# A normalisation of queries and keys moved from GpSimd to ScalarE: power -0.5 as a logarithm and an exponential

## The reference

```
def _layer(x, wqkv, qs, ksc, wo, lg, lb, w1, b1, w2, b2):
    h = shift_token(x)
    qkv = h @ wqkv
    q, k, v = jnp.split(qkv, 3, axis=-1)
    q, k, v = (to_heads(q), to_heads(k), to_heads(v))     # 8 heads of 64
    q = l2norm(q) * qs
    k = l2norm(k) * ksc
    q, k = rotary_xpos(q, k)
    o = local_attention(q, k, v)                          # windows of 64, looks one back
    x = x + o @ wo
    h = layernorm(shift_token(x))
    a, g = jnp.split(h @ w1 + b1, 2, axis=-1)
    return x + (a * gelu(g)) @ w2 + b2
```

## Time and profile before

| | |
|---|---|
| median of 3 runs | 2177.14 us (2174.58 to 2178.0) |
| profiled execution | 2163.13 us |
| its span, first to last instruction | 2161.4 us |
| granted TensorE clock, mean | 0.977 |
| busy: PE, DVE, ACT, POOL | 1991.7, 1773.1, 1369.1, 1233.1 us |

### The profile page before, as it was taken

One profiled execution on the slowest core, in us unless ns is written; L12 is line 12 of the kernel. 1 busy time (PEld: TensorE's weight loads), 2 busy tenths in 40 slices (PEclk: granted clock), 3 DMA queues, 4 the chain that ended last, 5 costly groups with the idle time before them and its releaser, 6 DMA issues. The chain is left out here.

```text
span 2161.4 us, 45576 instructions
## 1 busy us (share of the span) xinstructions
PE 1991.7 (92%) x16998; PEld 1090.6 (50%) x16998; DVE 1773.1 (82%) x2383; ACT 1369.1 (63%) x3435; POOL 1233.1 (57%) x599
## 2 busy tenths in 40 slices
PE   6687899999999999789999999967999999999997
PEld 2233555555555555345444444434555555555553
DVE  6986798998999997458888888547998998999983
ACT  8454566667667666336676766745666667666663
POOL 0217777777877775434122222257777777777760
PEclk9799999999999999999999999989999999999999
DMA  2004111211111210242322222022211111111111
GB/s 64 0 1 119 43 36 36 47 38 36 45 39 32 46 36 21 71 121 66 90 51 51 51 51 51 15 82 64 49 37 36 45 40 31 45 41 35 41 31 44
DMA packets 85473, 101.38 MB, mean 47 GB/s; under 512 B 13504, under 2 KB 60552, under 8 KB 83208
## 3 DMA queue, kind: packets, MB, share of 16 engines
q1 hardware_dynamic: 82824, 96.77, 17.9%
q10 hardware_dynamic: 2432, 1.70, 0.3%
HBM read 33.94 MB, written 10.49 MB: 21 GB/s over the span
## 5 line engine op out<-in xcount | busy, mean ns | idle before, releaser
L848 POOL TENSOR_TENSOR ffn_RN<-ffn_SS,ffn_mhalf 128x16 f32<-128x16 f32 x128 | 372.5, 2910 | 274.2 <-DVE ffn_SS L794 273.8
L842 POOL TENSOR_TENSOR ffn_QK<-ffn_T 128x1024 f32<-128x1024 f32 x128 | 420.2, 3283 | 18.3 <-DVE ffn_T L742 18.1
L2004 DVE TENSOR_REDUCE attn_b_NX<-attn_b_s 128x1 f32<-128x512 f32 (+3 forms) x608 | 368.9, 657 | 74.9 <-PE attn_b_s L1696 69.8
L589 ACT ACTIVATE ffn_PB<-ffn_s,ffn_NM 128x128 f32<-128x128 f32 x1024 | 360.6, 390 | 101.0 <-DVE ffn_NM L764 101.0
L1922 ACT ACTIVATE attn_b_PT<-attn_b_s 128x1024 f32<-128x1024 f32 (+1 forms) x320 | 286.9, 943 | 131.9 <-PE attn_b_s L1730 131.6
L633 ACT ACTIVATE ffn_SQ<-ffn_w 128x1024 f32<-128x1024 f32 x128 | 131.1, 1024 | 308.0 <-DVE ffn_T L742 307.7
L836 POOL TENSOR_TENSOR ffn_PB<-ffn_PB,ffn_RDEN 128x1024 f32<-128x1024 f32 x128 | 243.7, 1904 | 25.9 <-DVE ffn_RDEN L727 25.9
L378 PE MATMUL ffn_w<-ffn_Wqkv,ffn_H 128*128 128x512 f32 x512 | 244.5, 600 | 9.2 <-ACT ffn_SQ L633 5.6
L589 ACT ACTIVATION_READ_ACCUMULATOR ffn_PB<-ffn_s,ffn_NM 128x1 f32 x1024 | 236.5, 231 | 0.0
L1696 PE MATMUL attn_b_s<-attn_b_KS,attn_b_QS 62*128 62x512 f32 (+3 forms) x768 | 231.8, 402 | 0.0
L758 DVE TENSOR_TENSOR ffn_QK<-ffn_QK,ffn_RN 128x1024 f32<-128x1024 f32 x128 | 221.4, 1730 | 0.4 <-POOL ffn_RN L848 0.3
(11 more groups left out here) (250 smaller groups left out, 3760.5 us busy)
## 6 DMA issues: line engine op xcount, KB each, us to landing
ffn_Voff<-ffn_Vcur SPq DMA_DIRECT2D x248, 128.0 KB, 2.3
ffn_H<-ffn_Y SPq DMA_DIRECT2D x64, 128.0 KB, 2.5
ffn_H<-ffn_U SPq DMA_DIRECT2D x64, 128.0 KB, 2.5
attn_b_QS<-attn_b_qk_parts SPq DMA_DIRECT2D x64, 128.0 KB
attn_b_KS<-attn_b_qk_parts SPq DMA_DIRECT2D x64, 128.0 KB
attn_b_qk_parts<-attn_b_RP SPq DMA_DIRECT2D x6, 1024.0 KB, 9.7
ffn_rope<-in_ffn_rope_dram SPq DMA_DIRECT2D x4, 1024.0 KB, 8.0
attn_b_rope<-attn_b_OS SPq DMA_DIRECT2D x252, 16.0 KB
```

What stands on the lines that cost most here:

```text
L589: last = act.activation(PB[:, x % 2, e, p, :], s_ps[:, e, p * P:(p + 1) * P], ACT.Exp, bias=NM[:, x % 2, e, p:p + 1], accum_out=DEN[:, x % ...
L842: pool.tensor_tensor(QK[:, x % 2, :, :, :].rearrange("p c q k -> p (c q k)"), T1[:, :, :, :].rearrange("p c h k -> p (c h k)"), T2[:, :, : ...
L848: pool.tensor_tensor(RN[:, x % 2, :], SS[:, x % 2, :], mhalf[:, :], ALU.pow).then_inc(rnorm, 1)
L2004: dve.tensor_reduce(at, bank, AX_X, ALU.max, negate=True).then_inc(s1_read, 1)
```

## The change

The constant tile `mhalf` and its memset are gone. GpSimd's power is replaced by two activations on ScalarE, a logarithm from SS into RN and an exponential with scale -0.5 in place. They stand behind the QT copy of the step, wait for `clamped` and for the release of the RN buffer (`scaled`), and a new semaphore `lnsum` orders the second after the first. The counts for which others wait on `s_zero` are one lower.

```diff
-        mhalf = sb("mhalf", [P, 2 * NH])
...
+        lnsum = sem("lnsum")
...
-                    sp.wait_ge(s_zero, 3)
+                    sp.wait_ge(s_zero, 2)
...
                     act.activation(QT[:, x % 2, :, :], w1_ps[:, 0, :].rearrange("p (q c) -> p q c", c=P), ACT.Copy)\
                        .then_inc(qt, 1)
+                if real(i + 2):
+                    x = i + 2
+                    act.wait_ge(clamped, x + 1)
+                    if x >= 2:
+                        act.wait_ge(scaled, x - 1)
+                    act.activation(RN[:, x % 2, :], SS[:, x % 2, :], ACT.Ln).then_inc(lnsum, 1)
+                    act.wait_ge(lnsum, x + 1)
+                    act.activation(RN[:, x % 2, :], RN[:, x % 2, :], ACT.Exp, scale=-0.5).then_inc(rnorm, 1)
...
-                        dve.wait_ge(s_zero, 2)
+                        dve.wait_ge(s_zero, 1)
...
-            pool.memset(mhalf[:, :], -0.5).then_inc(s_zero, 1)
...
-            pool.wait_ge(s_zero, 3)
+            pool.wait_ge(s_zero, 2)
...
                                        T2[:, :, :, :].rearrange("p c h k -> p (c h k)"), ALU.add).then_inc(rope_sum, 1)
-                    pool.wait_ge(clamped, x + 1)
-                    if x >= 2:
-                        pool.wait_ge(scaled, x - 1)
-                    pool.tensor_tensor(RN[:, x % 2, :], SS[:, x % 2, :], mhalf[:, :], ALU.pow).then_inc(rnorm, 1)
```

## The result

The changed kernel takes 2247.96 us in the median of five runs (2243.06 to 2255.75), the kernel before, run beside it, 2174.58 (2167.83 to 2178.0). The ratio is 1.0346, with a 95% interval of 1.0314 to 1.0377: **3.5% slower**, 73 us. The forecast was 2240.5 us, 2.9% slower, with a range of 2208 to 2262. In the changed kernel the lines behind the edit have moved by seven or eight: the scaling of queries and keys is L766 (was L758), the rotary add L849 (L842), the multiply of the probabilities L843 (L836), the input normalisation's product L685 (L677), the clamp of the sum of squares L802 (L794). L670 and L672 are the logarithm and the exponential.

The account below looks back on a forecast made before the run. TensorE and VectorE, with hardly any slack between them, were taken to bound the kernel. 28 x (1.22 + 0.88 + 0.45) = 71.4 us, less 8, gave +63.4; with 14 us from profiled to plain runs, 2240.5 us; range 2208 to 2262.

Parts of the forecast that it names:

- The heart of it: Without the power, L836 runs early and L842 starts before the scaling L758, which then ends 1.08 us behind it.
- D: Fourth of four repeating steps (i % 4 = 3): L842 starts before L758, whose end comes 0.88 us later.
- B: Second of four repeating steps (i % 4 = 1): L842 starts before L758, whose end comes 1.22 us later.
- The delays pass through: TensorE's L397 and gate matmul L453 already wait for VectorE, so the delays of B and D count in full.
- Rival 2: TensorE covers VectorE's delays: partly, 2225 or 2211 us, 8 in 100; wholly, 2182 us, 2 in 100.
- The pair in A: ScalarE's two activations delay the gelu's table load after D, into step i % 4 = 0: 0.45 us.
- rival 3: The two activations bring two table loads behind every QT copy: 72 us more, 2312 us; 3 in 100.
- The steady sum: 28 groups of four steps, each longer by 1.22 + 0.88 + 0.45 us: 71.4 us.
- Start and end of each stage: First and last steps, with no L691 or L749 before L758: between 0 and -12 us, taken as -8.
- so those L758 only gain: In a stage's first and last steps no L691 or L749 precedes L758, so it only gets shorter; term -8 us.
- cost zero as long as L742 is later than the pair: In steps i % 4 = 0, 1, 2 ScalarE has idle time behind the pair, so it costs zero there.
- Rival 1: VectorE keeps its turn, as L842 starts after L758 in B and D: -34.6 us, 2142.5 us; 7 in 100.

Follow-up runs that it names:

- e4_neither: The kernel before with neither GpSimd's power nor ScalarE's pair, the factors set to one once: 2219.41 us, ratio 1.0233.
- e5_swap: The changed kernel with VectorE's scaling moved ahead of its neighbour (L757 or L699) in D and B: 2175.42 us, ratio 1.0033.
- e1_turn: The changed kernel with a wait: GpSimd starts a tile's add only after the scaling of the tile before: 2172.68 us, ratio 1.002.
- e3_both: The kernel before with ScalarE's pair added and used, GpSimd's power kept but its result unread: 2189.13 us, ratio 1.0085.
- e2_turn_norm: e1_turn with ScalarE's pair moved behind the two activations of the input normalisation: 2166.39 us, ratio 0.998.

## Why the prediction was right, and where it was off

- **The heart of it, that L836 gets out of the way and the add takes VectorE's turn, holds.** L843 starts 0.09 us after L735's end in D; the add runs 2.36 us and starts 0.07 to 0.08 behind L750; the handover of 1.08 us from one row of the kernel before repeats (1.08 to 1.09 us in all 56 scalings that meet an add in the changed kernel). Terms: B +1.22 forecast, +1.25 measured; D +0.88 and +0.90. e4_neither shows 2.14 for the two with the pair absent, e5_swap and e1_turn show that it is the turn and nothing else.
- **By the Trainium skill (SBUF — State Buffer, Who interferes with whom) issue order decides who is blocked, and for the whole instruction.** The traces agree in each direction: 0.44 us of lead for GpSimd make the scaling 3.00 us, 0.16 us of lead for VectorE (e5_swap) make it 1.22 and the add 3.26.
- **The delays pass through.** TensorE's wait for the scaling in B is 1.47 us (1.4 forecast), for the product of D 1.06 (1.1 forecast). Rival 2, in which TensorE covers them, is refuted in this direction.
- **The pair in A.** 0.45 us forecast, 0.35 to 0.40 measured in the changed kernel, 0.35 to 0.50 in e3_both. The two take 0.21 and 0.22 us, as the line through the earlier trace rows said, and overlap the QT copy's end a little. L772's wait in A rose from 0.56 to 1.14 us: 0.35 for the pair, and 0.22 because the scaling before it is shorter (1.43 to 1.21). No table load was added: rival 3 is refuted.
- **The steady sum.** 28 times 2.50 is 70.0 us; forecast 71.4.
- **The mis-sized term is "Start and end of each stage", -8 us.** Inside the stages the profiles differ by 79.5 us; less the steady 70.0 that is +9.5. The step that failed is "so those L758 only gain", taken as all that changes there. They do gain: those of the first seven steps take 1.21 or 1.22 us. But I costed the pair in A to D of the steady state only, "cost zero as long as L742 is later than the pair". In the first steps the input normalisation stands behind the pair, and that is the case which the step of costing left out: it is on VectorE's path. e2_turn_norm against e1_turn gives this 4.5 us in a start at full clock; the blocked clamp adds 0.9 us. The forecast also took the clock as it was: the three falls in each start of the changed kernel cost some 4.6 us, where the kernel before has one. That the longer waits bring the falls is likely and not shown; each kernel has one profiled execution. A queue that a moved step is put ahead of has to be read at the start of a stage too, not just in its repeating part.
- **Rival 1's price was wrong.** It said 2142.5 us if VectorE kept its turn. e1_turn and e5_swap are that case, and take 2172.68 and 2175.42. The shorter scalings save VectorE's time, but four steps stay at 41.4 us, because the next waits, for TensorE's L499 in D and L544 behind B, are right behind. Here the delays passed in full and the gains did not: TensorE's 41.14 busy us of 41.40 in the earlier trace rows hinted at that, and the forecast applied it to rival 2 alone.
- **The step from profile to median.** I added 14 us for the gap between the profiled execution and the median. The change is better seen as a difference: 63.4 us forecast, 73.4 measured in the medians. Against the profiled 79.5 us inside the stages, the term of the starts and ends is 17.5 too low and the steady one 1.4 too high; the medians then lie 6 us below that, which no row explains. So it is in part luck that the total of 2240.5 us came within 8 of the measured one.
- **The bounds.** Taken to their extremes, the terms as given reach from 2218 to 2256 us, not from 2222 to 2262. The measured 2247.96 lies in both.

Left open: why, between the stages and with the same code, the clock stands at 0.50 for 38 us in one profiled execution and for 65 us in another; and whether the falls in the starts come in every execution.

## What to carry to other kernels

Taking work off an engine with slack can cost time when two engines exclude each other, as VectorE and GpSimd do here: what runs after it moves forward and takes a turn that another engine needed more. Look in the timeline at who starts first on each side of the removed instruction, and keep the turn, with a wait or by swapping neighbours, before counting a gain. An instruction that waits for another engine belongs behind the ready work of its queue, and that has to be checked in the first steps of a stage as well as in the steady ones. Before the microseconds of such a start are shared out among causes, its granted clock has to be read step by step.

## What the runs showed of the hardware

- A two-input VectorE instruction of 1.21 us that meets a GpSimd one of the same kind in progress ends 1.08 us behind that one's end, whatever its own start (1.08 to 1.09 us in all 56 cases of the changed kernel): it lasts 3.00, 2.95 or 3.41 us by how early it came. Its recorded duration has the wait in it, so VectorE looks busy (39.16 us of 43.90) while it stands.
- A small instruction can be held too: the clamp of 128x16 took 1.14 us in the place of 0.17 when the GpSimd instruction beside it had still 1.1 us to run.
- With TensorE's clock at 0.50 for 3.4 us, two matmuls of 128x512 took 1.69 us in the place of 1.02, and the step became 1.5 us longer.
- A 128x16 activation took 0.22 us as an exponential, and 0.20 to 0.31 us as a logarithm.
